# New places in the unit for the copy of the block ends and most other work of a Mamba scan stage

## The chip, the cores and the metric

The kernel runs on one core of a Trainium2 chip. The metric is the device time of one execution in microseconds. The core's engines each work through a queue of their own in order: PE (TensorE, matmuls), DVE (VectorE), ACT (ScalarE), POOL (GpSimd) and SP (SyncE, which issues DMAs here). They meet at semaphores.

## The reference

The input is (4, 2048, 256). A Mamba layer and a mixture of experts follow one another, each with a residual and a layer norm. The change is in the Mamba layer. Per batch, with 512 inner channels and 16 states:

```python
xz = x @ in_proj_w.T + in_proj_b;  x_in, z = split(xz)
x_conv = silu(causal_conv4(x_in) + conv_b)
dt_low, B, C = split(x_conv @ x_proj_w.T)          # 64, 16, 16
dt = softplus(dt_low @ dt_proj_w.T + dt_proj_b)
A_bar = exp(dt * A);  B_bar = (A_bar - 1) / A * B  # A = -exp(A_log)
h = A_bar * h + B_bar * x_conv                     # over 2048 positions
y = (sum_s h * C + D * x_conv) * silu(z)
x = layernorm(x + y @ out_proj_w.T + out_proj_b)
```

Then each token's router scores choose two of 16 experts.

## The kernel before, in words

The scan stage runs over 16 units. A unit is 512 positions of one batch; the state `h` is carried between units of the same batch. The 512 channels are 4 chunks of 128 partitions. A unit has 64 items, one for each chunk and state, in 32 pairs: pair `i`, half `e` is chunk `i // 16 * 2 + e`, and the state follows from `i % 16`. Item number `m = 2 i + e` is also the step of the unit. Each engine's program is a loop over `m` from 0 to 63; in each step it emits the item's fixed work and then whatever the tables put there. The tables are the whole schedule: no planner runs, and an instruction placed at a step waits by semaphore until its inputs are there, holding up all that is behind it on its engine.

There are two kinds of pairs (`KINDS`). For kind `d`, ACT makes `a_ps = exp(dt*A)` (`make_a`, L766), POOL makes `h = x_conv*b_rep` (`make_u`, L656), DVE multiplies the two (`make_b`, L1205) and scans (L1221). For kind `f`, PE makes the increments from turned rows and step matrices (`make_du`, L1050, four 128-column products a half) into the only `g_ps`, DVE corrects the starts of the four blocks of 128 (`join`, L1214) and scans (L1229). Then `hc = h*c_rep` is made on POOL (L673, one pair later) or, for three of 16 pairs, on DVE (L1239). PE adds it into `y_ps` two pairs later (`add_item`, L1028).

Beside its items a unit makes the next one's inputs, tile by tile, through the two PSUM banks `work`; the tiles take turns in the order of `PLACE`, and a tile waits until the one before it in its bank has been copied out. `x0` to `x3` and `z0` to `z3` are the input projection, `c0` to `c3` the convolution, `low` and `bc` are dt_low, B and C, `d0` to `d3` the dt projection, `T0` to `T3` turned `x_conv`, `r` the skip term, `o` the output projection of the unit before, `t`, `lg`, `pf` its transposition, logits and slot numbers. PE makes a tile at its step in `PLACE` (a part a step); ACT copies it one step after its last part (DVE for `r` and `o`). Softplus is Abs and Relu of a `d` tile, Sigmoid (`Z_AT`), Square and two polynomials in `g_ps` (`SQUARES_AT` on ACT, `LOGS_AT` on DVE), and an addition (`ADD_RELU_AT` on POOL), in two groups of two chunks; `PAUSE` is where the kinds leave `g_ps` free for it.

The block ends: B's rows leave `low` for DRAM (`store_rows` at SP step `BC_OUT_AT`), and come back spread over the partitions as `b_rep` and `c_rep`, as `b_part` and `c_part`, and as `b_end`, the ends of the four blocks (`load_parts` at `PARTS_AT`, L527 to L531). ACT copies `b_end` with its sign changed (`turn_ends`, L793, at `TURN_AT`), POOL multiplies it (`ENDS_AT`) for the joins of the next unit, and `both` (`BOTH_AT`) from the parts for the skip term. SP's program steps once a pair and issues the `c_rep` load of the pair after next when `hc` of two pairs ago is done. The load of the next unit's `x_t` waits for the gate (`GATE_AT`, Silu of all `z`).

Of the kernel before, what the change touches and what calls it, by code (L numbers as in the profile page):

```python
# [168 lines left out]
def mamba(nc, d):  # L169
# [5 lines left out]
    with ExitStack() as ctx:  # L175
        def sb(name, shape, dt=F32):
            return ctx.enter_context(nc.sbuf_tensor(name, shape, dt))
# [50 lines left out]
        low = sb("low", [RANK + 2 * NS, T])  # L228
# [108 lines left out]
        def pool_slot(s):  # L337
# [11 lines left out]
        NEXT = ["x0", "x1", "x2", "x3", "c0", "c1", "c2", "c3", "low", "bc", "d0", "d1", "T0", "T1", "z0", "z1"]  # L349
        OWN = ["d2", "d3", "T2", "T3", "r0", "r1", "r2", "r3", "z2", "z3"]  # L350
        ROUTING = ["o0", "o1", "t0", "t1", "lg", "pf"]
        PLACE = [("x0", 0), ("x1", 0), ("d2", 2), ("d3", 3), ("c0", 6), ("c1", 6), ("T2", 10), ("T3", 14), ("o0", 16), ("o1",
# [3 lines left out]
        U_AT = [-4, -1, None, 3, None, 6, 9, None, 10, None, 15, 17, 18, None, 24, None, 28, 32, None, 34, None, 38, 39, None,  # L356
                42, None, 47, 51, 53, None, 56, None]
        A_AT = [-2, 1, -1, 4, 6, 6, 9, 11, 11, 14, 16, 17, 19, 21, 27, 26, 29, 31, 31, 35, 37, 41, 42, 44, 44, 45, 51, 53, 55,
                56, 58, 57]
        DU_AT = [None, None, 2, None, 6, None, None, 10, None, 13, None, None, None, 24, None, 27, None, None, 34, None, 38,  # L360
                 None, None, 43, None, 48, None, None, None, 56, None, 58]
        SCATTER_AT = (1, 2, 4, 6, 9, 12, 13, 16)
        ADD_RELU_AT = (58, 63, 24, 26)
        Z_AT = (49, 5)
        STEPS_AT = (47, 48, 54, 57, 58, 61)
        SUMS_AT = (23, 24)
        SILU_AT = (12, 36)
        SQUARES_AT = ((51, 54, 55), (12, 18, 21))
        LOGS_AT = ((54, 55), (22, 24))
        TURN_AT, ENDS_AT, BOTH_AT = 45, 55, 49  # L370
        MAX_AT, INDEX_AT, IDS_AT, CHOOSE_AT, CANDIDATES_AT, REDUCE_AT, PLACES_AT, NOTED_AT = 45, 48, 50, 52, 55, 55, 59, 62
        ROOT_AT, INVERSE_AT, NORMALISE_AT = 24, 26, 28
        GATE_AT, HALO_IN_AT, HALO_OUT_AT = 59, 5, 61
        SKIP_AT = (25, 29, 35, 39)
        TOKENS_AT, ROWS_OUT_AT, BC_OUT_AT, PARTS_AT = 9, 23, 21, 23
        WHERE = dict(PLACE)
        ORDER = {t: n for n, (t, _) in enumerate(PLACE)}

# [3 lines left out]
        class Plan:  # L382
# [3 lines left out]
            def __init__(self, kinds, offset, per=0):  # L386
                self.tiles = [t for t, _ in PLACE if t in kinds]
                self.offset, self.per = offset, per
# [26 lines left out]
        last = Plan(OWN + ROUTING, AHEAD + INNER * (UNITS - 1))  # L415
        assert INNER % 2 == 0 and len(PLACE) == INNER
        assert min(WHERE["T0"], WHERE["T1"]) > WHERE["pf"]
# [154 lines left out]
        def _(pool):  # L572
# [85 lines left out]

            U_PLACE = sorted((U_AT[i] + e, i, e) for i in range(PAIRS) for e in range(2) if plain(i))

# [41 lines left out]
            def unit_program(u, plan):  # L702
                for m in range(ITEMS):
# [17 lines left out]
                    if m == ENDS_AT and plan is not last:  # L721
                        find_ends(u)
                    if m in ADD_RELU_AT:
                        c = ADD_RELU_AT.index(m)
                        if c >= 2:
                            add_relu(u, c)
                        elif plan is not last:
                            add_relu(later(u), c)
                    if plan is not second and m in SCATTER_AT:
                        scatter(u, SCATTER_AT.index(m))  # L730

# [13 lines left out]
        def _(act):  # L745
# [4 lines left out]

            A_PLACE = sorted((A_AT[i] + e, i, e) for i in range(PAIRS) for e in range(2))

# [173 lines left out]
            def weave(u, plan, m):  # L926
# [11 lines left out]
                for t in plan.whole_at(m - 1):  # L938
                    if t[0] != "o":
                        tile(u, plan, t)  # L940
                if plan.has("c0") and m in SILU_AT:
                    half = 2 * SILU_AT.index(m)
                    emptied_all(act, plan, u, [f"c{c}" for c in (half, half + 1)])
# [4 lines left out]
                if plan.has("d2"):  # L948
                    if m == Z_AT[1]:
                        find_z(u, 1)  # L950
                    if m in SQUARES_AT[1]:
                        squared(u, 1, SQUARES_AT[1].index(m))
                if plan.has("d0"):
                    if m == Z_AT[0]:
                        find_z(n, 0)
                    if m in SQUARES_AT[0]:
                        squared(n, 0, SQUARES_AT[0].index(m))
                    if m == TURN_AT:
                        turn_ends(u)
                    if m in STEPS_AT:  # L960
                        make_steps(u, plan, STEPS_AT.index(m))
                if m == GATE_AT:
# [41 lines left out]
        def _(pe):  # L1004
# [132 lines left out]

            DU_PLACE = [(DU_AT[i] + e, i, e) for i in range(PAIRS) for e in range(2) if not plain(i)]

# [28 lines left out]
        def _(dve):  # L1168
# [158 lines left out]
            def weave(u, plan, m):  # L1327
# [15 lines left out]
                if plan.has("o0"):  # L1343
                    if m in SUMS_AT:
                        norm_sums(u, plan, f"o{SUMS_AT.index(m)}")
                    if m == INVERSE_AT:
# [814 lines left out]
```

## Time and profile before

| what | us |
|---|---|
| median of 3 runs (2834.14 to 2836.39) | 2834.33 |
| the profiled execution | 2841.85 |
| its span, first to last instruction | 2840.0 |
| scan stage, up to about | 2425 |
| mean granted clock of TensorE, share of full | 0.956 |

The page gives the busy time of each engine; a timeline lists single instructions with the idle time of their engine before them and what ended it. The stage after 2425 us (the experts) is not touched.

### The profile page before, as it was taken

The numbers are of one execution on the slowest core, as the hardware profiler recorded it, in microseconds if no ns is written. First come the engines' busy times: TensorE is split into PE (matmuls) and PEld (weight loads), VectorE is DVE, ScalarE is ACT, GpSimd is POOL, SyncE is SP. The second block draws the span as 40 slices with busy tenths as digits, with TensorE's granted clock in tenths as the row PEclk, the third lists the DMA queues.
The fourth block names the chain that finished last, engine by engine and source line by source line (L and its number), as shares of the span: only waits on it lengthen the run. The fifth ranks groups of instructions, "written<-read, shape, count | busy, mean of one in ns | idle before, by whom it ended". The sixth has DMA issues, their size and how long they took to land. (4 is left out here: it accounts for less than half of the span.)

```text
span 2840.0 us, 37945 instructions
## 1 busy us (share of the span) xinstructions
PE 2558.9 (90%) x9658; PEld 1453.0 (51%) x9659; DVE 2363.1 (83%) x3895; ACT 1800.2 (63%) x3530; POOL 2284.4 (80%) x2094
## 2 busy tenths in 40 slices
PE   6889999999999999999898989898989988499997
PEld 2445554545454545455454545454545444377764
DVE  3889898989898989989897989898989889366668
ACT  5676766767676768585867676767676754133348
POOL 1889898979798989898998989898989898255553
PEclk8999999999999999999999999999999988699998
DMA  3333333433344333334333343434333332766557
GB/s 85 93 106 119 100 120 102 124 100 125 95 121 110 113 113 113 115 110 115 110 108 109 110 112 113 115 115 107 119 108 119 99 111 89 208 186 185 183 185 248
DMA packets 248306, 349.34 MB, mean 123 GB/s; under 512 B 75575, under 2 KB 123323, under 8 KB 247612
## 3 DMA queue, kind: packets, MB, share of 16 engines
q1 hardware_dynamic: 231372, 301.41, 36.4%
q0 software_dynamic: 15600, 44.79, 4.5%
q10 hardware_dynamic: 1152, 1.06, 0.2%
q8 instruction: 71, 1.16, 0.2%
q14 instruction: 111, 0.91, 0.1%
HBM read 288.72 MB, written 58.45 MB: 122 GB/s over the span
## 5 line engine op out<-in xcount | busy, mean ns | idle before, releaser
L673 POOL TENSOR_TENSOR hc<-h,c_rep 128x512 f32<-128x512 f32 x832 | 1053.1, 1271 | 165.9 <-PE y_ps L1028 87.7
L1028 PE MATMUL y_ps<-hc,dg_inv 128*128 128x512 f32 x1664 | 870.2, 616 | 25.2 <-POOL hc L673 22.3
L656 POOL TENSOR_TENSOR h<-x_conv,b_rep 128x512 f32<-128x512 f32 x640 | 807.6, 1271 | 86.5 <-DVE h L1221 60.1
L1221 DVE TENSOR_TENSOR_SCAN h<-a_ps,carry,h 128x512 f32<-128x512 f32 x640 | 807.0, 1272 | 12.6 <-ACT score L824 10.5
L766 ACT ACTIVATE a_ps<-dt,a_mat 128x512 f32<-128x512 f32 x640 | 436.5, 685 | 482.9 <-DVE h L1221 469.0
L1050 PEld LDWEIGHTS g_ps<-b_steps,x_conv_rows 128*128 128x128 f32 x3072 | 411.2, 199 | 278.3 <-issue 278.3
L1205 DVE SCALAR_TENSOR_TENSOR h<-a_ps,h 128x512 f32<-128x512 f32 x640 | 429.7, 672 | 72.2 <-ACT a_ps L766 65.8
L1050 PE MATMUL g_ps<-b_steps,x_conv_rows 128*128 128x128 f32 x3072 | 431.2, 285 | 45.6 <-DVE h L1229 17.8
L1028 PEld LDWEIGHTS y_ps<-hc,dg_inv 128*128 128x128 f32 x1664 | 291.2, 194 | 309.8 <-issue 203.8
L766 ACT ACTIVATE h<-dt,a_mat 128x512 f32<-128x512 f32 x384 | 269.9, 711 | 2.1 <-POOL hc L673 1.4
L1103 PE MATMUL work<-x_in,dg_tap 128*128 128x512 f32 x512 | 250.0, 593 | 1.9 <-ACT x_in L894 1.1
L1229 DVE TENSOR_TENSOR_SCAN g_ps<-g_ps,carry,h 128x512 f32<-128x512 f32 x192 | 246.8, 1286 | 5.4 <-ACT h L766 0.8
L1229 DVE TENSOR_TENSOR_SCAN h<-g_ps,carry,h 128x512 f32<-128x512 f32 x192 | 245.1, 1277 | 3.8 <-ACT h L766 0.3
L1720 POOL DMA_INDIRECT y_planes<-gathered,home x144 | 139.8, 971 | 132.0 <-DVE gathered L2051 120.4
L1028 PE MATMUL y_ps<-hc,ident 128*128 128x512 f32 x384 | 203.1, 619 | 8.0 <-DVE hc L1239 8.0
L1090 PE MATMUL work<-x_t,w_in 128*128 128x512 f32 x256 | 136.5, 641 | 44.1 <-DMA x_t<-in_x_t 30.8
L1214 DVE TENSOR_TENSOR g_ps<-g_ps,minus_u 128x6 f32<-128x6 f32 x192 | 31.4, 163 | 154.9 <-PE g_ps L1050 148.2
L1851 PE MATMUL banks<-w_up,gathered 128*128 x576 | 150.3, 384 | 0.0
L1239 DVE SCALAR_TENSOR_TENSOR hc<-g_ps,a_inv,c_rep 128x512 f32<-128x512 f32 x192 | 142.5, 742 | 0.0
L1114 PE MATMUL work<-low,dt_out 64*128 64x512 f32 x128 | 87.9, 772 | 60.4 <-ACT dt L866 58.9
L638 POOL DMA_INDIRECT slot_rows<-x_tok,place x120 | 121.5, 1013 | 25.0 <-issue 12.3
L1103 PEld LDWEIGHTS work<-x_in,dg_tap 128*128 128x128 f32 x512 | 91.0, 190 | 89.2 <-issue 87.5
(248 smaller groups left out, 3622.7 us busy)
## 6 DMA issues: line engine op xcount, KB each, us to landing
c_rep<-bc_rows SPq DMA_DIRECT2D x512, 256.0 KB, 3.4
b_rep<-bc_rows SPq DMA_DIRECT2D x320, 256.0 KB, 3.7
gathered<-slot_rows SPq DMA_DIRECT2D x144, 129.5 KB, 2.2
gathered<-y_planes SPq DMA_DIRECT2D x32, 512.0 KB, 5.6
x_t<-in_x_t SPq DMA_DIRECT2D x16, 512.0 KB, 5.0
x_tok<-in_x_tok SPq DMA_DIRECT2D x16, 512.0 KB, 4.9
out<-mixed_rows SPq DMA_DIRECT2D x16, 512.0 KB, 3.1
x_t_rows<-y_gated SPq DMA_DIRECT2D x15, 512.0 KB, 5.7
```

What stands on the lines that cost most here:

```text
L656: nc.gpsimd.tensor_tensor(h[:, i % SLOTS, e], x_conv[:, u[1] % 2, chunk(i, e)], b_rep[:, n % BS], ALU.mult).then_inc(u_ready, 1)
L673: nc.gpsimd.tensor_tensor(hc[:, i % HCS, e], h[:, i % SLOTS, e], c_rep[:, i % CS], ALU.mult).then_inc(hc_pool, 1)
L766: nc.scalar.activation(out, dt[:, c], ACT.Exp, scale=a_mat[:, c, s:s + 1]).then_inc(made, 1)
L1028: nc.tensor.matmul(y_ps[:, e], by, hc[:, i % HCS, e], start=first_one, stop=(i % HALF == HALF - 1)).then_inc(summed, 1)
L1050: one = nc.tensor.matmul(g_ps[:, e, k * P:(k + 1) * P], x_rows[:, c, k], b_steps[:, f, k], start=True, stop=True)
L1103: mm = nc.tensor.matmul(out, dg_tap[:, c, k], x_in[:, c, k:k + T], start=(k == 0), stop=(k == TAPS - 1))
L1205: nc.vector.scalar_tensor_tensor(out=slot, in0=a_ps[:, e], scalar=1.0, in1=slot, op0=ALU.subtract, op1=ALU.mult).then_inc(b_ready, 1)
L1221: nc.vector.tensor_tensor_scan(slot, a_ps[:, e], slot, before_it, ALU.mult, ALU.add).then_inc(scanned, 1)
L1229: nc.vector.tensor_tensor_scan(out, g_ps[:, e], slot, before_it, ALU.add, ALU.mult).then_inc(scanned, 1)
L1239: nc.vector.scalar_tensor_tensor(out=hc[:, i % HCS, e], in0=g_ps[:, e], scalar=a_inv[:, c, s:s + 1], in1=c_rep[:, i % CS], op0=ALU.mult, o ...
L1720: nc.gpsimd.indirect_dma_start(d["y_planes"], bass.IndirectOffsetOnAxis(home[:, c:c + 1], 0), y_slots[:, c], None).then_inc(y_stored[c // ...
L1851: one = nc.tensor.matmul(gu_ps[:, c % 2, 0:2 * IF], xt[:, c % 4, h * P:(h + 1) * P], w_up[:, e, h], start=(h == 0), stop=(h == KT - 1))
```

## The change

No work is added or removed. The tables that say at which step of the unit an operation is emitted get other numbers: `PLACE` for PE's tiles and so their order in the two banks, `U_AT`, `A_AT`, `DU_AT` for the operands of the pairs, and nearly every single step. With them go the waits.

```diff
-        PLACE = [("x0", 0), ("x1", 0), ("d2", 2), ("d3", 3), ("c0", 6), ("c1", 6), ("T2", 10), ("T3", 14), ("o0", 16), ("o1",
-                 17), ("x2", 22), ("r0", 24), ("x3", 25), ("r1", 26), ("c3", 27), ("c2", 31), ("r2", 34), ("t0", 36), ("t1", 36),
-                 ("r3", 39), ("low", 39), ("lg", 40), ("d1", 46), ("bc", 46), ("d0", 47), ("z2", 50), ("pf", 52), ("z1", 52),
-                 ("z3", 54), ("z0", 54), ("T0", 61), ("T1", 61)]
-        U_AT = [-4, -1, None, 3, None, 6, 9, None, 10, None, 15, 17, 18, None, 24, None, 28, 32, None, 34, None, 38, 39, None,
-                42, None, 47, 51, 53, None, 56, None]
-        A_AT = [-2, 1, -1, 4, 6, 6, 9, 11, 11, 14, 16, 17, 19, 21, 27, 26, 29, 31, 31, 35, 37, 41, 42, 44, 44, 45, 51, 53, 55,
-                56, 58, 57]
-        DU_AT = [None, None, 2, None, 6, None, None, 10, None, 13, None, None, None, 24, None, 27, None, None, 34, None, 38,
-                 None, None, 43, None, 48, None, None, None, 56, None, 58]
-        SCATTER_AT = (1, 2, 4, 6, 9, 12, 13, 16)
-        ADD_RELU_AT = (58, 63, 24, 26)
-        Z_AT = (49, 5)
-        STEPS_AT = (47, 48, 54, 57, 58, 61)
-        SUMS_AT = (23, 24)
-        SILU_AT = (12, 36)
-        SQUARES_AT = ((51, 54, 55), (12, 18, 21))
-        LOGS_AT = ((54, 55), (22, 24))
-        TURN_AT, ENDS_AT, BOTH_AT = 45, 55, 49
-        MAX_AT, INDEX_AT, IDS_AT, CHOOSE_AT, CANDIDATES_AT, REDUCE_AT, PLACES_AT, NOTED_AT = 45, 48, 50, 52, 55, 55, 59, 62
-        ROOT_AT, INVERSE_AT, NORMALISE_AT = 24, 26, 28
-        GATE_AT, HALO_IN_AT, HALO_OUT_AT = 59, 5, 61
-        SKIP_AT = (25, 29, 35, 39)
-        TOKENS_AT, ROWS_OUT_AT, BC_OUT_AT, PARTS_AT = 9, 23, 21, 23
+        PLACE = [("x0", 1), ("x1", 1), ("c0", 4), ("c1", 4), ("T3", 7), ("d3", 9), ("T2", 11), ("d2", 11), ("o0", 14), ("o1",
+                 18), ("x2", 22), ("r0", 25), ("x3", 25), ("r1", 27), ("c3", 29), ("c2", 30), ("t1", 35), ("t0", 36), ("r2", 37),
+                 ("low", 39), ("r3", 43), ("bc", 44), ("lg", 44), ("d0", 47), ("d1", 48), ("z1", 50), ("pf", 51), ("z0", 52),
+                 ("z3", 54), ("T0", 56), ("z2", 58), ("T1", 62)]
+        U_AT = [-3, -1, None, 0, None, 6, 9, None, 10, None, 15, 20, 22, None, 24, None, 27, 31, None, 33, None, 36, 38, None,
+                42, None, 47, 50, 51, None, 56, None]
+        A_AT = [-3, 1, 1, 3, 4, 7, 10, 13, 12, 15, 17, 18, 22, 24, 26, 25, 29, 33, 33, 36, 39, 40, 42, 43, 46, 47, 50, 53, 55,
+                55, 57, 58]
+        DU_AT = [None, None, 2, None, 5, None, None, 11, None, 14, None, None, None, 24, None, 29, None, None, 34, None, 38,
+                 None, None, 44, None, 48, None, None, None, 57, None, 59]
+        SCATTER_AT = (1, 2, 5, 6, 8, 9, 14, 15)
+        ADD_RELU_AT = (57, 58, 26, 29)
+        Z_AT = (50, 14)
+        STEPS_AT = (47, 48, 55, 57, 62, 63)
+        SUMS_AT = (22, 24)
+        SILU_AT = (17, 34)
+        SQUARES_AT = ((51, 54, 55), (16, 19, 20))
+        LOGS_AT = ((54, 55), (22, 23))
+        TURN_AT, ENDS_AT, BOTH_AT = 52, 55, 48
+        MAX_AT, INDEX_AT, IDS_AT, CHOOSE_AT, CANDIDATES_AT, REDUCE_AT, PLACES_AT, NOTED_AT = 48, 49, 50, 51, 54, 56, 59, 62
+        ROOT_AT, INVERSE_AT, NORMALISE_AT = 29, 29, 30
+        GATE_AT, HALO_IN_AT, HALO_OUT_AT = 60, 1, 60
+        SKIP_AT = (25, 26, 39, 43)
+        TOKENS_AT, ROWS_OUT_AT, BC_OUT_AT, PARTS_AT = 8, 23, 23, 24
```

## Rows read from the trace of the kernel before

**Rows 1.** The page: busy us (share of the span) and instructions of each engine.

```profile
PE 2558.9 (90%) x9658; PEld 1453.0 (51%) x9659; DVE 2363.1 (83%) x3895; ACT 1800.2 (63%) x3530; POOL 2284.4 (80%) x2094
```

**Rows 2.** Windows of a unit: length, busy PE, PEld, DVE, ACT, POOL, clock, DMA.

```profile
212.30:359.80 147.50, 138.47 (x507) 74.32 (x506) 130.59 (x185) 103.19 (x197) 131.09 (x118) 0.97 0.38 112
...
950.10:1097.60 147.50, 137.80 (x509) 74.31 (x508) 130.80 (x184) 103.15 (x197) 130.87 (x118) 0.98 0.38 112
```

**Rows 3.** The line of the root: durations in ns, first and last start.

```profile
L891 ACT ACTIVATE spread<-spread x15: 205/205/208, 267.6 to 2333.4; 128x4 f32<-128x4 f32 x15
```

**Rows 4.** Table of waits, whole span: us in total, times, longest.

```profile
DVE g_ps L1214 <- PE g_ps L1050: 148.2, 51, 9.7
...
PE work L1090 <- DMA x_t<-in_x_t: 30.8, 14, 2.3
```

**Rows 5.** Timeline of DVE, one unit: start, us, instruction, idle before.

```profile
1015.45 0.17 DVE L1214 TENSOR_TENSOR g_ps<-g_ps,minus_u 128x6 f32<-128x6 f32 x1 [0.74 <-PE g_ps L1050]
...
1049.32 1.28 DVE L1221 TENSOR_TENSOR_SCAN h<-a_ps,carry,h 128x512 f32<-128x512 f32 x1 [0.70 <-ACT score L824]
...
1056.32 1.26 DVE L1221 TENSOR_TENSOR_SCAN h<-a_ps,carry,h 128x512 f32<-128x512 f32 x1
1065.58 0.17 DVE L1214 TENSOR_TENSOR g_ps<-g_ps,minus_u 128x6 f32<-128x6 f32 x1 [8.00 <-PE g_ps L1050]
...
1093.47 0.69 DVE L1205 SCALAR_TENSOR_TENSOR h<-a_ps,h 128x512 f32<-128x512 f32 x1 [2.42 <-ACT a_ps L766]
...
1095.92 0.69 DVE L1205 SCALAR_TENSOR_TENSOR h<-a_ps,h 128x512 f32<-128x512 f32 x1 [0.55 <-ACT a_ps L766]
```

**Rows 6.** Timeline of PE in the same unit.

```profile
1051.32 1.12 PE L1114 MATMUL work<-low,dt_out 64*128 64x512 f32 x2
...
1057.84 2.07 PE L1114 MATMUL work<-low,dt_out 64*128 64x512 f32 x2 [3.35 <-ACT dt L866]
...
1090.12 2.74 PE L1028 MATMUL y_ps<-hc,dg_inv 128*128 128x512 f32 x6
1095.18 1.96 PE L1090 MATMUL work<-x_t,w_in 128*128 128x512 f32 x4 [2.32 <-DMA x_t<-in_x_t]
```

**Rows 7.** Timeline of ACT in the same unit.

```profile
1051.27 0.70 ACT L766 ACTIVATE h<-dt,a_mat 128x512 f32<-128x512 f32 x1
1055.71 0.22 ACT L793 ACTIVATE b_minus<-b_end 128x24 f32<-128x24 f32 x1 [3.74 <-DMA b_end<-bc_rows]
...
1062.40 1.28 ACT L872 ACT_TABLE_LOAD   x1
1063.69 1.15 ACT L872 ACTIVATE x_arg<-x_arg,shifts 128x1024 f32<-128x1024 f32 x1
...
1087.88 1.91 ACT L966 ACTIVATE gate<-gate 128x2048 f32<-128x2048 f32 x1
...
1095.19 0.69 ACT L766 ACTIVATE a_ps<-dt,a_mat 128x512 f32<-128x512 f32 x1 [0.66 <-POOL dt L700]
```

**Rows 8.** Timeline of SP's DMA issues in the same unit.

```profile
1049.82 0.67 SPq L531 DMA_DIRECT2D b_end<-bc_rows  x1
...
1089.89 0.43 SPq L540 DMA_DIRECT2D x_t<-in_x_t  x1
```

**Rows 9.** Of the tile `b_end`: from issue to landing.

```profile
DMA to landing us min/median/max: 4.1/5.8/7.1
```

**Rows 10.** Window of the slow stretch, columns as in rows 2.

```profile
1057.80:1063.40 5.60, 5.56 (x12) 3.02 (x13) 0.00 (x0) 5.24 (x14) 5.60 (x6) 0.50 0.08 28
```

**Rows 11.** Timeline of POOL in the same unit.

```profile
1050.68 1.27 POOL L673 TENSOR_TENSOR hc<-h,c_rep 128x512 f32<-128x512 f32 x1 [0.46 <-DVE h L1221]
...
1093.90 1.26 POOL L700 TENSOR_TENSOR dt<-dt,poly 128x512 f32<-128x512 f32 x1
```

**Rows 12.** Groups of instructions in the window of rows 2: count, busy us, mean ns.

```profile
L673 POOL TENSOR_TENSOR hc<-h,c_rep 128x512 f32<-128x512 f32 x52 | 65.8, 1272 | 9.7 <-PE y_ps L1028 5.2 <-DVE h L1221 2.2 <-DVE h L1229 2.0
...
L1205 DVE SCALAR_TENSOR_TENSOR h<-a_ps,h 128x512 f32<-128x512 f32 x40 | 26.9, 671 | 4.1 <-ACT a_ps L766 3.8 <-POOL h L656 0.4
```

## The prediction

> **What bounds the kernel now.** I read the page's busy shares first [rows 1]: no engine is full, but three stand close together. The reader sees that more sharply in the windows of one unit [rows 2]: of 147.5 us, PE is busy 137.8, POOL 130.9, DVE 130.8 and ACT 103.2, and the other full units are within 3 us of that. A unit takes (2333.4 - 267.6) / 14 = 147.56 us, by the one square root in each [rows 3]; 64 steps, so 2.3 us a step. The scans sit on DVE and need all that the others make, so what a unit could lose is DVE's idle time, some 17 us of it.
>
> Then the table of waits [rows 4], to see who DVE waits for. One wait stands out: the join of the block starts (L1214) on PE, 148 us in total. The unit's timeline of DVE [rows 5] shows that it is one hole: after a scan at 1056.32 nothing until the join of pair 25 at 1065.58, 8.00 us idle. A second hole is at the unit's end, 2.42 and 0.55 us for `a_ps` (steps 62, 63). The rest are waits below 0.8 us.
>
> Back from the first hole: PE's timeline [rows 6] has `d0` at 1057.84, 3.35 us idle before it, waiting for ACT's copy of `d1` (same bank). ACT [rows 7] ends an exponential at 1051.97 and then sits 3.74 us until `b_end` has landed, because its copy, `TURN_AT` 45, is ahead of the copy of `d1` in its queue. SP [rows 8] could issue that load only at 1049.82, behind the store of `low`, and it takes 5.8 us to land (median, [rows 9]). Then comes a second price: the granted clock is 0.50, so 1.2 of 2.4 GHz [rows 10], and a product takes 2.07 us instead of 1.12; so PE's pairs of records in 1057.8 to 1063.4 give back 2.8 us late. Idle and slow clock together are 6.2 of the 8.0 us.
>
> **What the change takes away.** (a) `TURN_AT` 52. Its load moves too: the store goes from SP step 21 to 23, the parts from 23 to 24. SP gets to 24 when POOL has made `hc` of pair 22, which was 1050.68 + 1.27 = 1051.95; with two issues ahead `b_end` goes out near 1053.6 and lands near 1059.5. DVE's step 50 would without the hole begin at 1057.6, so the copy at step 52 comes 2 us or more after the landing. `low` is copied in step 43 as before, and `d0`, now ahead of `d1`, waits only for `bc`, copied at 45. POOL's `both` (now 48) needs the parts landed: POOL has three 1.27 us operations between, so 0 to 1.3 us of wait, in POOL's own idle time; I take 0. Removed: 8.00 us a unit. (b) `add_relu` of chunk 1 moves from POOL step 63, which ended at 1095.16 [rows 11] just ahead of ACT's exponential for pair 0 [rows 7], to 58, and `softplus` stays at 55: the 2.97 us at the unit's end go. (c) In steps 24 to 44 PE had no idle time and was late: DVE has six small waits there, 0.18 to 0.74 us, the largest for `du` of pair 15, 2.13 us in all (that one in [rows 5]). Now `softplus` ends one DVE step earlier (23 instead of 24), ahead of the sums of `o1`, so PE starts `du` of pair 13 some 5 us earlier against DVE. I take all 2.13. Together 13.1 us.
>
> **What it adds.** PE's steps are priced by its rows: an item or one 128x512 product 0.86 us (six records in 2.74, less 0.16 of overlap), a `du` 0.9, four transposes 0.45, `d` 1.05; DVE's by a scan 1.2 and a `make_b` 0.6 (mean duration less overlap) [rows 6, 12].
> 1. The gate goes to step 60, behind `z2` made at 58. SP loads `x_t` only after it (0.1 us after the Silu in the old order, [rows 7, 8]), 5.0 us to landing. From the scan of pair 29: 4.4 us of ACT, then 5.4, makes 9.8; DVE reaches step 0 after 7. `x0`, `x1` now stand at step 1, ahead of `du` of pair 2, and delay PE so that join 4 is late by 1.35 us. It was 2.3 us of harmless PE idle time [rows 4]. Bounds 0 and 2.8 (no step of lead).
> 2. `c0`, `c1` at 4, `T3` 7, `d3` 9, `T2`, `d2` 11. After `du` 4 PE has 13.4 us of work up to the end of `du` 7 (steps 11, 12 instead of 10, 11), DVE 11.3 us from join 4 to join 7; in the old order PE had 10.9. So 2.1 us. `T3` also waits for the copy of `c0`, which ACT makes in step 8; PE comes there as late as that. Bounds 0 (if PE keeps a lead) and 4.
> 3. ACT in steps 14 to 18: Sigmoid, Square, Silu and four table loads, 12 us against DVE's 9.6; join 7's wait gives ACT most of that. 0.3, bounds 0 and 2.4.
> 4. Root at ACT 29, inverse at DVE 29 (24 and 26 before). The root stands behind an exponential that waits for the scan of pair 14: 0.7 + 1.28 + 0.2 us after it, where DVE has one scan of 1.2 to do. 1.15 us; bounds 0 and 2.3.
> 5. At steps 48 to 50 PE has `d1` (1.05) between the halves of `du` 25, and it comes late: steps 24 to 47 hold 24 items, 10 halves of `du`, 14 products of `x`, `c` and `low`, `r0` to `r3`, `d0`, transposes, `bc` and `lg`, so PE is at step 48 about 51.7 us after the `softplus` of step 23, while DVE ends the scan of pair 23 after 50.0 (24 scans, 15 `make_b`, 4 `hc`, 5 joins, the sums of `o1`, four skips, two gated chunks, term 4). Join 25: 1.5 us, bounds 0 and 3. `MAX_AT` 48 waits for `lg`'s scores, made in ACT step 48, as before at 45 [rows 5]: 0.75 for 0.70.
> 6. Index 49, ids 50, choose 51, `pf` 51 stand back to back (before 48, 50, 52, 52): POOL waits about 2 us for the index, ACT's choose ends 4.8 us after it, PE waits 0.5 to 2.2 us at `pf`. Behind it are only items and `z` tiles; PE is then some 1 us ahead at join 29. 0 at full clock; upper bound in rival A.
> `SCATTER_AT` spreads over 1 to 15 instead of 1 to 16, POOL's 1.27 us operations [rows 12] are less crowded at 15 to 19: I take nothing.
> Sum: 1.35 + 2.1 + 0.3 + 1.15 + 1.5 + 0.05 = 6.45; with 13.1 removed, -6.65 a unit. Fifteen units have it (the last makes nothing for a next one), so -100; the prologue's copy no longer stands ahead of `d0`: -3. The profiled execution took 2841.85 us (1.85 beside its span of 2840.0), so it would take 2739. It is 7.5 over the median of the runs; from the median, 2834.3 - 103 = 2731.
>
> The trace bears on term 4: a table load starts at 1062.40 and its activation at 1063.69, 1.29 us for a switch [rows 7]. The Trainium skill ("ScalarE: Activation LUTs", *What ACT_TABLE_LOAD costs*) gives a switch 1283 ns for the load and another 1380 ns of drain. The load agrees, the drain isn't seen; by the page term 4 would be 2.5 us and the time some 20 us longer (an estimate from that page), 2752.
>
> **Rivals.**
> A. PE's new pause at `pf` or at `T3` makes the clock fall as after `d0`. For: that pause was 3.35 us, the new ones together reach 2 to 3. Against: after the 2.32 us before `x0` PE ran at full speed, four records in 1.96 us [rows 6]. Price 2.8 us for a slow stretch like [rows 10] and 1 for what it holds: -2.85 a unit, 2788.
> B. Slower. `x0` and `x1` stand ahead of `du` 2 and 4, and SP's `x_t` behind a gate one step later. If ACT comes to the gate 4.5 us or more later than I take, PE idles 6 us at `x0` and comes out at half clock: 4.5 + 2.8 = 7.3 us eats the gain. At three steps (6.9 us) of lateness it is 9.7 - 6.65 = +3.05 a unit, 2877. For: ACT's queue has carry, `z2`, load and Silu in one step. Against: ACT has the least work of the four.
> C. The copy still waits, since its load was moved too. It then holds ACT 3.7 us again, now ahead of pair 27's exponential: -2.95 a unit, 2787.
> D. The new waits overlap or vanish: -10.5 a unit, 2673. POOL's 130.9 us a unit would allow it.
> E. The idle time only moves: 2834.
>
> **Chances.** Forecast 0.54, A 0.17, B 0.12, C 0.06, D 0.08, E 0.03. A measurement of this kernel tells 0.2% (6 us) from no change. Faster 0.85, same 0.03, slower 0.12. The forecast's own range is 2700 to 2765; with A and C it is 2680 to 2800, which leaves out B, E and most of D.
>
> **What would show it.** A unit of 141 us by the roots; no idle time before the copy of the block ends; no half-clock stretch once a unit; DVE's wait before join 25 under 3 us; no `a_ps` wait over 1 us in steps 62 and 63. New: waits before joins 4 and 7, and before the inverse (L1288). I am wrong if the copy waits for its load, if the clock is low once a unit at another place, or if `x_t` holds PE by more than 4 us.

## The result, and the profile after

The changed kernel takes 2873.63 us (median of 4 runs, 2869.80 to 2874.85) beside 2835.36 for the kernel before on the same chip: ratio 1.0132, 95% interval 1.0114 to 1.0149. It is slower by 38 us; the prediction was 2731, with a range of 2680 to 2800. The profiled execution took 2873.16 us, its span 2871.3.

"Join 25" is the join of pair 25, "the softplus" DVE's first operation on the polynomials in `g_ps` (L1323, step 54), and PE's "pause" is idle time of PE in front of an instruction.

The page's busy line of after, which answers to [rows 1]: the number of instructions is the same on each of these engines, and PE's busy time is 24 us longer.

```profile
PE 2583.0 (90%) x9658; PEld 1464.8 (51%) x9659; DVE 2359.6 (82%) x3895; ACT 1808.6 (63%) x3530; POOL 2285.2 (80%) x2094
```

The line of the root (durations in ns, first and last start), for [rows 3]:

```profile
L891 ACT ACTIVATE spread<-spread x15: 205/207/208, 274.6 to 2377.3; 128x4 f32<-128x4 f32 x15
```

A unit is (2377.3 - 274.6) / 14 = 150.19 us, 2.63 longer than before where 6.65 less was forecast. Before the first root 7.0 us were added and after the last 12.6 taken away; five steps of that are the root's own new place. 7.0 + 14 x 2.63 - 12.6 = 31.3 is the difference of the spans. The prologue did gain: DVE's first scan starts at 62.5 in place of 69.5, so 7 us where 3 were forecast.

The timeline of DVE over one unit, those lines that have idle time before them (start, us, instruction, idle before and what ended it), for [rows 5]:

```profile
976.33 0.22 DVE L1237 TENSOR_SCALAR carry<-g_ps,minus_u 128x1 f32<-128x1 f32 x1 [0.72 <-PE y_ps L1028]
984.45 0.17 DVE L1214 TENSOR_TENSOR g_ps<-g_ps,minus_u 128x6 f32<-128x6 f32 x1 [1.59 <-PE g_ps L1050]
992.66 0.69 DVE L1205 SCALAR_TENSOR_TENSOR h<-a_ps,h 128x512 f32<-128x512 f32 x1 [0.61 <-ACT a_ps L766]
997.04 0.69 DVE L1205 SCALAR_TENSOR_TENSOR h<-a_ps,h 128x512 f32<-128x512 f32 x1 [2.48 <-ACT a_ps L766]
...
1019.61 0.69 DVE L1257 TENSOR_TENSOR skip<-work,x_conv 128x512 f32<-128x512 f32 x1 [1.65 <-PE work L1119]
1025.83 0.18 DVE L1288 RECIPROCAL spread<-spread 128x4 f32<-128x4 f32 x1 [1.16 <-ACT spread L891]
...
1059.74 0.17 DVE L1214 TENSOR_TENSOR g_ps<-g_ps,minus_u 128x6 f32<-128x6 f32 x1 [0.49 <-PE g_ps L1050]
1063.95 1.28 DVE L1221 TENSOR_TENSOR_SCAN h<-a_ps,carry,h 128x512 f32<-128x512 f32 x1 [0.36 <-ACT score L824]
1068.71 0.17 DVE L1214 TENSOR_TENSOR g_ps<-g_ps,minus_u 128x6 f32<-128x6 f32 x1 [1.29 <-PE g_ps L1050]
1073.16 0.69 DVE L1205 SCALAR_TENSOR_TENSOR h<-a_ps,h 128x512 f32<-128x512 f32 x1 [1.17 <-ACT a_ps L766]
1077.46 0.69 DVE L1205 SCALAR_TENSOR_TENSOR h<-a_ps,h 128x512 f32<-128x512 f32 x1 [0.46 <-ACT a_ps L766]
1084.58 1.22 DVE L1323 SCALAR_TENSOR_TENSOR poly<-g_ps,x_arg 128x1024 f32<-128x1024 f32 x1 [3.88 <-ACT g_ps L887]
1101.74 0.69 DVE L1205 SCALAR_TENSOR_TENSOR h<-a_ps,h 128x512 f32<-128x512 f32 x1 [2.33 <-ACT a_ps L766]
```

The hole of 8.00 us before join 25 is gone, 1.29 is left. In its place stand many smaller waits, above all 3.88 us before the softplus (step 54), 2.33 at the unit's end and 2.48 at step 19. With two of 0.21 us they are 18.6 us, against 15.2 counted in the same way before. Of these 3.4 us the unit shows 2.63, since DVE was also busy for 0.8 us less ([rows 2] and the windows below).

Back from the 3.88 us. The timeline of ACT:

```profile
1068.68 1.28 ACT L872 ACT_TABLE_LOAD   x1
1069.97 1.15 ACT L872 ACTIVATE x_arg<-x_arg,shifts 128x1024 f32<-128x1024 f32 x1
1071.14 1.28 ACT L766 ACT_TABLE_LOAD   x1
...
1074.78 0.31 ACT L923 ACTIVATE chosen<-y_gated 128x128 bf16<-128x128 f32 x1
...
1082.86 0.69 ACT L853 ACTIVATE gate<-work,b_in 128x512 f32<-128x512 f32 x1 [4.69 <-PE work L1094]
1083.44 1.11 ACT L887 ACTIVATE g_ps<-square,shifts 128x1024 f32<-128x1024 f32 x1
```

and the timeline of PE in the same stretch:

```profile
1075.23 0.68 PE L1010 MATMUL work<-ahead,dt_out 1*128 1x80 f32 x2 [3.20 <-ACT chosen L923]
...
1076.29 2.06 PE L1028 MATMUL y_ps<-hc,dg_inv 128*128 128x512 f32 x2
1078.14 1.91 PE L1094 MATMUL work<-x_t,w_in 128*128 128x512 f32 x2
```

The Sigmoid with its two table loads stands on ACT ahead of the chosen tokens, PE waits 3.20 us for these at `pf`, and comes out of the pause at the lower of its two clocks, 1.2 of 2.4 GHz: an item takes 2.06 us in place of 1.02. ACT waits 4.69 us for `z0`, and the squared term in `g_ps` (L887) that the softplus needs is queued behind that copy. In the kernel before, the pause at `pf` was 0.3 to 1.6 us (14.4 us over 15 times). A second pause sits before `x2`, which waits for DVE's norm sum:

```profile
1005.80 1.13 PE L1090 MATMUL work<-x_t,w_in 128*128 128x512 f32 x2 [3.46 <-DVE x_tok L1272]
1006.76 1.73 PE L1028 MATMUL y_ps<-hc,ident 128*128 128x512 f32 x2
```

The windows of the unit and of both stretches (busy PE, PEld, DVE, ACT, POOL; then the granted clock), for [rows 2, 10]:

```profile
953.94:1104.13 150.19, 139.14 (x507) 74.90 (x508) 129.96 (x184) 103.42 (x197) 130.41 (x118) 0.97 0.37 110
1075.20:1083.40 8.20, 8.17 (x22) 4.02 (x23) 5.05 (x7) 3.51 (x8) 3.15 (x5) 0.58 0.23 78
1005.80:1010.20 4.40, 4.40 (x7) 1.90 (x8) 4.36 (x9) 2.67 (x6) 2.83 (x3) 0.63 0.10 34
```

The table of waits over the span (us in total, times, longest) shows that both are in every unit:

```profile
ACT gate L853 <- PE work L1094: 63.7, 14, 4.7
...
PE work L1090 <- DVE x_tok L1272: 48.2, 14, 3.5
```

### The profile page after: what moved, and what is told of

Read it like the earlier page. It is cut to its first block and busy times, and to the rows that moved or that the text cites. A ratio compares the mean times of both kernels' runs of the same rounds, so it can differ in the third digit from the quotient of the medians.

```text
span 2871.3 us, 37946 instructions
## 1 busy us (share of the span) xinstructions
PE 2583.0 (90%) x9658; PEld 1464.8 (51%) x9659; DVE 2359.6 (82%) x3895; ACT 1808.6 (63%) x3530; POOL 2285.2 (80%) x2094
## 3 DMA queue, kind: packets, MB, share of 16 engines
q8 instruction: 71, 1.16, 0.2%
## 5 line engine op out<-in xcount | busy, mean ns | idle before, releaser
L1028 PE MATMUL y_ps<-hc,dg_inv 128*128 128x512 f32 x1664 | 884.5, 623 | 40.2 <-POOL hc L673 24.1
L1050 PEld LDWEIGHTS g_ps<-b_steps,x_conv_rows 128*128 128x128 f32 x3072 | 403.1, 195 | 240.7 <-issue 236.9
L1028 PEld LDWEIGHTS y_ps<-hc,dg_inv 128*128 128x128 f32 x1664 | 299.7, 197 | 343.6 <-issue 210.0
L1050 PE MATMUL g_ps<-b_steps,x_conv_rows 128*128 128x128 f32 x3072 | 418.4, 280 | 26.3 <-DVE carry L1237 13.6
L1103 PE MATMUL work<-x_in,dg_tap 128*128 128x512 f32 x512 | 244.2, 596 | 2.9 <-ACT x_in L837 2.9
L1028 PE MATMUL y_ps<-hc,ident 128*128 128x512 f32 x384 | 221.0, 661 | 16.9 <-DVE hc L1239 16.5
L1090 PE MATMUL work<-x_t,w_in 128*128 128x512 f32 x256 | 147.7, 685 | 74.2 <-DVE x_tok L1272 48.2
L1094 PE MATMUL work<-x_t,w_in 128*128 128x512 f32 x256 | 147.8, 664 | 0.9 <-ACT dt L866 0.9
L784 ACT ACTIVATE carry<-h,minus_u 128x1 f32<-128x1 f32 x192 | 45.9, 286 | 157.5 <-DVE h L1229 157.5
```

Source lines behind the costliest of these rows:

```text
L1028: nc.tensor.matmul(y_ps[:, e], by, hc[:, i % HCS, e], start=first_one, stop=(i % HALF == HALF - 1)).then_inc(summed, 1)
L1050: one = nc.tensor.matmul(g_ps[:, e, k * P:(k + 1) * P], x_rows[:, c, k], b_steps[:, f, k], start=True, stop=True)
L1090: mm = nc.tensor.matmul(out, w_in[:, k, m * P:(m + 1) * P], x_t[:, nq, k], start=(k == 0), stop=(k == KT - 1))
L1094: mm = nc.tensor.matmul(out, w_in[:, k, m * P:(m + 1) * P], x_t[:, src, k], start=(k == 0), stop=(k == KT - 1))
L1103: mm = nc.tensor.matmul(out, dg_tap[:, c, k], x_in[:, c, k:k + T], start=(k == 0), stop=(k == TAPS - 1))
```

## The experiments

Medians are of 4 to 10 runs; ratios are to the kernel before, measured beside each (2834.0 to 2834.9), with their 95% interval. B is the kernel before, A the kernel after. Some edits are shown shortened to the numbers that change. Waits of DVE are those of one middle unit, where nothing else is said; the units of one execution are not all alike.

**The copy of the block ends alone (B).**

```diff
-        TURN_AT, ENDS_AT, BOTH_AT = 45, 55, 49
+        TURN_AT, ENDS_AT, BOTH_AT = 52, 55, 49
```

> The kernel before with one number changed: TURN_AT 45 becomes 52. If the 8.0 us hole before join 25 is the price of the copy that waits for its load (theory of the prediction, step a), some 7 to 8 us of each of 15 units go: 2720 us, no half-clock stretch once a unit. Rival: other waits stand right behind the hole (PE, POOL and ACT are each within 12% of the unit) and refill it: less than 3 us a unit, 2790 us or more.

2786.55 us, 0.9835 (0.9819 to 0.9852). The timeline of DVE where the hole was:

```profile
1031.80 0.17 DVE L1214 TENSOR_TENSOR g_ps<-g_ps,minus_u 128x6 f32<-128x6 f32 x1 [1.77 <-PE g_ps L1050]
1035.06 0.69 DVE L1205 SCALAR_TENSOR_TENSOR h<-a_ps,h 128x512 f32<-128x512 f32 x1 [1.75 <-ACT a_ps L766]
1046.94 1.23 DVE L1323 SCALAR_TENSOR_TENSOR poly<-g_ps,x_arg 128x1024 f32<-128x1024 f32 x1 [3.12 <-ACT g_ps L887]
```

The run gains 47 us, 7 of them in the prologue, and a unit is 144.58 us by the roots, 2.98 shorter. The unit shown is one of the long ones (145.4 us). The waits of 1.77 us (join 25) and 1.75 us (the exponential of pair 26) stand in all 14 units, but the one before the softplus is 3.1 to 3.2 us in three, 1.6 to 1.8 in ten and absent in one: 1.9 on average. So of a hole of 8.1 us on average (7.5 to 9.8) some 5.4 come back. PE now pauses 2.70 us at `pf`, where in the kernel before it paused 0.8 in the same unit: the pause at `pf` grows when the hole in front of it goes, with the table's numbers for `pf`, the Sigmoid and choose as they were. Its length is the same in every unit; what follows is not. In a unit with the long wait, then in the one without any:

```profile
1038.69 0.68 PE L1010 MATMUL work<-ahead,dt_out 1*128 1x80 f32 x2 [2.70 <-ACT chosen L923]
...
1039.75 2.05 PE L1094 MATMUL work<-x_t,w_in 128*128 128x512 f32 x2
...
896.27 0.41 PE L1010 MATMUL work<-ahead,dt_out 1*128 1x80 f32 x2 [2.69 <-ACT chosen L923]
...
896.91 1.10 PE L1094 MATMUL work<-x_t,w_in 128*128 128x512 f32 x2
```

The unit in which PE stayed at full clock has no wait before the softplus and took 142.4 us. As far as this one unit shows, what costs here is the slow clock behind the pause, and not the pause.

**`add_relu` alone (B).**

```diff
-        ADD_RELU_AT = (58, 63, 24, 26)
+        ADD_RELU_AT = (58, 59, 24, 26)
```

> The kernel before with one number changed: the addition of chunk 1 at POOL step 59 instead of 63. Step b of the prediction gave it the whole 2.97 us at the unit's end: 2790 us. Rival, from the trace read again: the first 2.42 us wait for ACT, which comes from the gate's Silu (1.91) and a table load (1.28) and not from POOL; only the 0.66 us before the second exponential are POOL's: 2826 us, and the 2.4 us wait in step 62 or 63 stays.

2860.04 us, 1.0097 (1.0080 to 1.0114): slower. The 0.55 us of step 63 went, the 2.42 of step 62 stayed at 2.41. The timeline of PE at the unit's end shows the cost:

```profile
1093.19 1.12 PE L1028 MATMUL y_ps<-hc,dg_inv 128*128 128x512 f32 x2 [0.77 <-POOL hc L673]
1096.75 3.75 PE L1090 MATMUL work<-x_t,w_in 128*128 128x512 f32 x4 [2.43 <-DMA x_t<-in_x_t]
```

POOL's extra 1.27 us at step 59 makes `hc` late, PE pauses for it, then 2.43 us for `x_t`, and the products of `x0` take 3.75 us; in the same unit before, after the pause for `x_t` alone, 1.96 [rows 6]. DVE then waits 2.68 us for PE's sum in `y_ps` (step 3) and 1.53 before join 4 (0.39 before). Both pauses are in all 14 units, but the slow clock is not: in six the four records of `x0` take 1.96 us. Between two roots there are 147.0 to 147.9 us where `x0` ran at full clock, 148.8 to 150.3 where it did not. In the kernel before, two of 14 units had a slow `x0` (3.65 us), with no pause for `hc` ahead.

**`pf` behind `z0` (A).**

```diff
-  ("z1", 50), ("pf", 51), ("z0", 52), ...   CANDIDATES_AT 54
+  ("z1", 50), ("z0", 51), ("pf", 53), ...   CANDIDATES_AT 55
```

> The changed kernel with pf at 53 behind z0 (at 51), and the candidates at 55. Theory: PE's 3.2 us pause at pf, for ACT's choose that stands behind Sigmoid and two table loads, drops the clock, z0 is late, ACT waits 4.7 us for it ahead of the Square, and softplus makes DVE wait 3.9 us. With two products in front of pf the pause is under 1 us, the clock stays up there, and 4 us a unit go: 2813 us. Rival: the Square is late through ACT's own queue, so DVE's wait before softplus stays over 3 us and the time within 10 us of 2873.

2814.95 us, 0.9936 (0.9917 to 0.9956), 58.7 below A, or 3.9 a unit. The pause at `pf` is 1.19 us and the item behind it takes 1.10; the wait of 3.88 is gone (those for pairs 26 and 27, 1.18 and 0.33, are not):

```profile
1056.91 0.44 PE L1010 MATMUL work<-ahead,dt_out 1*128 1x80 f32 x2 [1.19 <-ACT gate L853]
...
1057.58 1.10 PE L1028 MATMUL y_ps<-hc,ident 128*128 128x512 f32 x2
```

**The first Silu at 9 (A), alone and with `pf` at 53.**

```diff
-        SILU_AT = (17, 34)
+        SILU_AT = (9, 34)
```

> The changed kernel with the first Silu of x_conv at step 9 instead of 17. Theory: between steps 14 and 18 ACT has Sigmoid, Square, Silu and four table loads and is late for the exponentials of pair 10, DVE waits 0.6 and 2.5 us; with Silu and its two loads at a step where ACT is free these 3.1 us go: 2827 us. Rival: PE (join 7, x2) or POOL sets the pace in steps 14 to 24 and takes the time back: 2865 us or more.

2833.32 us, 0.9994 (0.9980 to 1.0007), 40.3 below A. Waits of 0.61 and 2.48 became 0.85, a new one of 1.97 stands at step 11, and PE's pause before `x2` fell to 1.1 us. Units took from 146.8 to 149.9 us. PE's timeline at `pf`, first in a unit of 149.8 us, then in one of 146.8:

```profile
1064.87 0.67 PE L1010 MATMUL work<-ahead,dt_out 1*128 1x80 f32 x2 [3.19 <-ACT chosen L923]
...
1065.92 2.05 PE L1028 MATMUL y_ps<-hc,dg_inv 128*128 128x512 f32 x2
...
1213.27 0.41 PE L1010 MATMUL work<-ahead,dt_out 1*128 1x80 f32 x2 [3.19 <-ACT chosen L923]
...
1213.91 1.10 PE L1028 MATMUL y_ps<-hc,dg_inv 128*128 128x512 f32 x2
1214.85 1.68 PE L1094 MATMUL work<-x_t,w_in 128*128 128x512 f32 x2
```

The pause is 3.19 us in both. In the first PE starts at half clock, in the second it falls back one item later (granted clock in the windows of the two stretches: 0.58 and 0.78), and the softplus waits 3.88 and 2.31 us. So of this wait some 1.6 us are the clock's and 2.3 are left without it, in A's order. The other difference between the two units is of the same kind, at step 35. Both have the pause of 1.01 us before the item there, and only the first a slow stretch behind it:

```profile
1028.23 1.13 PE L1028 MATMUL y_ps<-hc,dg_inv 128*128 128x512 f32 x2 [1.01 <-DVE y_gated L1251]
...
1031.83 1.91 PE L1050 MATMUL g_ps<-b_steps,x_conv_rows 128*128 128x128 f32 x8
...
1178.13 1.13 PE L1028 MATMUL y_ps<-hc,dg_inv 128*128 128x512 f32 x2 [1.01 <-DVE y_gated L1251]
...
1181.20 1.05 PE L1050 MATMUL g_ps<-b_steps,x_conv_rows 128*128 128x128 f32 x8
```

Joins 20 and 23 wait 1.00 and 1.21 us in the first unit, and only 0.50 (join 23) in the second: with the softplus 3.3 us of waits for the 3.0 of the units.

> The kernel after with both single edits together: pf at 53 behind z0 (alone 2815.0 us, 58.7 less than after) and the first Silu at 9 in place of 17 (alone 2833.3 us, 40.3 less). Theory (the two crowdings sit at different places of the unit and don't cover each other): they add, 2873.6 - 58.7 - 40.3 = 2775 us. Rival (one slack feeds both, PE's lead): 2805 to 2815 us. The unit with the Silu alone took 146.8 us in some units and 149.8 in others; if the clock after pf was what made the difference, the units here are all alike, near 143.3 us.

2797.91 us, 0.9868 (0.9851 to 0.9884): the Silu adds 17.0 us to `pf`'s gain, not 40.3. Between theory and rival. Alone the Silu's move had also brought the wait before the softplus from 3.7 to 2.8 us on average, for the clock fell later in many units, and the other edit removes that wait by itself; and the waits of 1.00 and 1.21 us at joins 20 and 23 are here too in some units (145.8 us, the others 144.3).

**The copy put back, with `pf` at 53 (A).**

```diff
-        TURN_AT 52, BC_OUT_AT 23, PARTS_AT 24
+        TURN_AT 45, BC_OUT_AT 21, PARTS_AT 23
```

> The kernel after with pf at 53, and the copy of the block ends put back: the copy at 45, SP's store of low at 21 and the load of the parts at 23. It tells what the copy is worth once nothing behind it waits. Theory (in the kernel before it was worth 3 us a unit of its 8.00, because the pause at pf took the rest): here the hole of 8 us comes back in full, less the waits that it covers (1.29 before join 25, 1.18 and 0.33 for exponentials behind it): 5.2 us a unit and the prologue's 7 us, so 2815 + 15 x 5.2 + 7 = 2900 us. Rival (the copy is worth 3 us a unit wherever it stands): 2815 + 48 = 2863 us.

2899.34 us, 1.0227 (1.0210 to 1.0244): 84.4 above the run without it. The theory had 85, but not by what happened: no hole of 8 us comes back before join 25. The copy now waits 7.28 us for its load, where it was 3.74 in B, and DVE pays 4.19 us of that at step 46, with 1.43 us for the scores (0.36 without the edit). The timeline of ACT:

```profile
1081.42 0.22 ACT L793 ACTIVATE b_minus<-b_end 128x24 f32<-128x24 f32 x1 [7.28 <-DMA b_end<-bc_rows]
```

In B the copy was worth 47 us. The two numbers don't measure one thing with and without the pause at `pf`: the edits differ (the store and the load go with the copy here) and so does the copy's own wait.

**Root, inverse and second skip put back (A).**

```diff
-        ROOT_AT, INVERSE_AT, NORMALISE_AT = 29, 29, 30    SKIP_AT[1] 26
+        ROOT_AT, INVERSE_AT, NORMALISE_AT = 24, 26, 28    SKIP_AT[1] 29
```

> The kernel after with pf at 53, and root, inverse and normalise put back to 24, 26 and 28 (after: 29, 29, 30), the second skip to 29 (after: 26). DVE's waits of 1.50 us for r1 (step 26) and of 1.16 us before the inverse (step 29) in a unit should go. Theory (each of these waits is paid in full): 2815 - 15 x 2.66 = 2775 us. Rival (PE is behind DVE in these steps, so that DVE, coming earlier, waits at the joins behind, pair 15 above all, for PE's du): 2800 to 2815 us, with a wait of 1 to 2.6 us before a join of steps 30 to 50.

With `pf` at 53: 2810.07 us, 0.9920 (0.9903 to 0.9936), 4.9 less. Waits of 1.50 and 1.16 us went, and 1.08 before the first skip and 2.40 before join 15 came. The rival's range.

> The kernel after with pf at 53, the first Silu at 9 (together 2797.9 us), and root, inverse, normalise at 24, 26, 28 and the second skip at 29. With the Silu at 17 that last step gave only 5 us (2815.0 to 2810.1) of the 40 that its waits held: DVE then waited 2.40 us before join 15, PE being late from a pause of 3.46 us before x2 and the half clock behind it. With the Silu at 9 that pause is 1.1 us and there is no half clock. Theory (PE's pause at x2 was what made it worthless): here the waits of 0.82 and 1.16 us are paid in full, 2797.9 - 15 x 1.9 = 2769 us. Rival (PE is late in steps 24 to 30 whatever the clock): 2790 to 2798 us, with 1.5 us or more before join 15.

With the Silu too: 2777.50 us, 0.9802 (0.9785 to 0.9819), 20.4 less. Without the Silu's move the table of waits has the line of A for the pause before `x2` (48.2 us, 14 times, longest 3.5); with it:

```profile
PE work L1090 <- DVE x_tok L1272: 15.3, 14, 1.1
```

Join 15 still waits 1.42 us, so 20 and not 28. The same edit was worth 0.3 us a unit while PE came late out of the pause at `x2`, and 1.4 once it did not.

**Copy at 52 and `pf` at 53 (B).**

```diff
-  ("z2", 50), ("pf", 52), ("z1", 52), ...   TURN_AT 45
+  ("z2", 50), ("z1", 52), ("pf", 53), ...   TURN_AT 52
```

> The kernel before with the copy of the block ends at 52 and pf moved from 52 (ahead of z1) to 53 (behind it). The run with the copy alone took 2786.6 us and had a new DVE wait of 3.12 us for ACT's Square (step 54) in each unit; behind it stood PE's pause of 2.70 us at pf for ACT's chosen tokens, and the half clock after it. Theory (the pause at pf is what ate the copy's 8.00 us): z1 covers 1.7 us of the pause, the clock stays up, the wait of 3.12 us goes: 2786.6 - 15 x 3.0 = 2741 us, and a unit of 141.0 us. Rival (the time only moves to the next late wait, of ACT's exponentials for pair 26, 1.75 us and growing): 2775 to 2790.

2763.31 us, 0.9748 (0.9731 to 0.9764), 23 below the copy alone. The wait before the softplus went in every unit, and 0.8 came back before join 4 in most. The waits of 1.77 and 1.75 us (join 25, pair 26) are unchanged: they have nothing to do with `pf`.

**Three more edits on top of that (B, copy 52, `pf` 53).**

The gate alone, the first two `b_steps` alone, and both.

```diff
-        GATE_AT, HALO_IN_AT, HALO_OUT_AT = 59, 5, 61
+        GATE_AT, HALO_IN_AT, HALO_OUT_AT = 57, 5, 61
```

```diff
-        STEPS_AT = (47, 48, 54, 57, 58, 61)
+        STEPS_AT = (52, 53, 54, 57, 58, 61)
```

> The kernel before with the copy at 52, pf at 53 (together 2763.3 us) and the gate's Silu at 57 in place of 59, so that SP's load of x_t goes out two steps earlier. In that run PE idled 2.40 us at x0 for the transfer of x_t, the eight products of x0 and x1 then took 4.7 us in place of 3.8, and DVE waited 1.19 us before join 4. Theory (x_t is late because the Silu is): PE's idle time at x0 goes, the clock stays up, join 4 waits under 0.4 us: 2763.3 - 15 x 0.8 = 2751 us, or 2739 if the a_ps waits of 2.42 and 0.81 us at the unit's end shrink too, being at other steps. Rival (ACT has no room at 57: the exponentials of pairs 29 to 31 wait for the Silu there, by as much as those of pair 0 did at 59): 2760 to 2770 us.

2828.49 us, 0.9967 (0.9953 to 0.9981), 65 slower than without it. `x_t` is in time, but the Silu with its loads now stands ahead of the exponential of pair 30. DVE waits 3.88 us for that and 3.33 at step 63 (2.42 and 0.81 before). The scan before the next `du` is late with it, and PE pauses 3.77 us and comes out at half clock:

```profile
1076.97 2.05 PE L1050 MATMUL g_ps<-b_steps,x_conv_rows 128*128 128x128 f32 x8 [3.77 <-DVE h L1229]
1078.81 3.55 PE L1028 MATMUL y_ps<-hc,dg_inv 128*128 128x512 f32 x4
```

> The kernel before with the copy at 52, pf at 53 (together 2763.3 us) and ACT's first two b_steps (1.28 us each) at 52 and 53 in place of 47 and 48. They stand ahead of the Sigmoid whose two table loads delay the exponential of pair 26, for which DVE waits 1.75 us in step 50. Theory (ACT's crowd of steps 47 to 51 sets that wait): the Sigmoid starts 1.3 to 2.5 us earlier, the wait of 1.75 goes or falls below 0.5: 2763.3 - 15 x 1.3 = 2744 us. Rival (ACT is as crowded at 52 to 54, with choose, the Square and the z copies): the wait reappears before the softplus or the exponential of pair 27, 2755 to 2770 us.

2762.22 us, 0.9751 (0.9732 to 0.9770): no change. The wait of 1.75 us fell to 0.59, but ACT's copy of a `z` tile is later, and PE's pause for it is now 2.08 us (1.2 before), followed by four products in 3.60 us:

```profile
1178.59 3.60 PE L1094 MATMUL work<-x_t,w_in 128*128 128x512 f32 x4 [2.08 <-ACT gate L853]
```

Join 29 then waits 1.27 us, where there was no wait. So 1.2 of the 1.75 us before pair 26 were those of two `b_steps` ahead of its exponential in ACT's queue.

> The two edits of the runs beside it together. Theory (they sit at different places of the unit): the gains add, 2763.3 - 12 - 19 = 2732 us, or 2720 if the gate's own waits shrink. Rival (PE, busy 137 of 143 us of a unit, is the bound once the waits are down to this): no unit under 142 us, 2750 us.

2825.52 us, 0.9974 (0.9963 to 0.9984): as with the gate alone.

**Who makes the 2.42 us at the unit's end.** The last `b_steps` from 61 to 63, in B alone, then on top of the copy, `pf` and the first two `b_steps`, and then with `ADD_RELU_AT[1]` 62 in place of 63.

```diff
-        STEPS_AT = (47, 48, 54, 57, 58, 61)
+        STEPS_AT = (47, 48, 54, 57, 58, 63)
```

> The kernel before with one edit: ACT's b_steps of step 61 (1.26 us, between the gate's Silu and the table load for the exponential of pair 0) at 63. The prediction put DVE's 2.42 us at the unit's end down to POOL's add_relu; moving that alone took away only the 0.55 us of step 63. Theory (the wait is ACT's chain of load, Silu, carries, b_steps, load): it falls by 1.27 to 1.15 us, 2834.3 - 15 x 1.27 = 2815 us if DVE is given it. Rival (x_t and PE set the start of the unit, DVE only waits elsewhere): 2828 to 2834 us, with the 1.27 us before join 4 or step 63.

2835.89 us, 1.0003 (0.9994 to 1.0013): no change. The wait at step 62 is 1.25 in place of 2.42, the one at 63 1.73 in place of 0.55.

> The kernel before with the copy at 52, pf at 53, the first two b_steps at 52 and 53 (together 2762.2 us) and the last b_steps at 63 in place of 61. Theory: the wait at step 62 falls by 1.27 us, 2762.2 - 19 = 2743 us. Rival (PE, coming from its wait for x_t, is late for join 4 by the same time): 2755 to 2762 us.

2760.86 us, 0.9732 (0.9716 to 0.9748): the same shift, 0.69 and 2.06 us.

> The same with POOL's add_relu of chunk 1 at 62 in place of 63: half 1 of pair 0's exponential waits 1.0 us for it. Theory (that wait is paid once the 2.42 us are shorter): 6 to 12 us below the run beside it, so 2734 us. Rival (an earlier add_relu delays hc on POOL and PE pauses for it just ahead of x_t, comes out at half clock, as with add_relu at 59 in the kernel before, which then took 2860.0 us): 2765 to 2785 us.

2750.99 us, 0.9706 (0.9690 to 0.9722), the best version found, 83 us below B and 123 below A. The timeline of DVE at the unit's end:

```profile
1052.98 0.69 DVE L1205 SCALAR_TENSOR_TENSOR h<-a_ps,h 128x512 f32<-128x512 f32 x1 [1.25 <-ACT a_ps L766]
```

The wait has two makers in a row: ACT's chain of Silu, `b_steps` and table load, and POOL's `add_relu` 1.2 us behind it. With ACT's part alone moved, the wait passed to POOL's and the time stayed; with POOL's moved as well 10 us went. POOL's at 62 without ACT's wasn't run. Join 4 is at 1.54 us now, so PE is next.

## Why the prediction was wrong

The ledger of a unit, from the two timelines of DVE. Forecast: 15.2 - 13.1 + 6.45 = 8.6 us of waits; measured 18.6.

| step of the prediction | forecast | measured |
|---|---|---|
| (a) copy | -8.00 | the wait gone, and the three below marked * in its place |
| (b) `add_relu` | -2.97 | -0.64 (2.33 is left) |
| (c) small waits, 24 to 44 | -2.13 | -1.71, and 1.65 for `r1` |
| 1. join 4 | +1.35 | none (0.39 before); 0.72 at step 10 |
| 2. join 7 | +2.1 | 1.59 |
| 3. ACT, steps 14 to 18 | +0.3 | 3.09, where 0.78 was |
| 4. root and inverse | +1.15 | 1.16, paid only if PE keeps up |
| 5. joins 23, 25*, score | +1.55 | 0.49, 1.29, and -0.34 for the score |
| 6. choose and `pf`* | 0 | 3.88 |
| no term: pairs 26, 27* | 0 | 1.63 |

The waits are 10 us a unit above the forecast. Of 12 us too much, 3.88 stand at the softplus and 1.63 at pairs 26 and 27, which the prediction had at nothing; 2.33 are left of step (b), 2.0 of step 3 and 2.1 of step (c). The other steps took 1.8 us less than forecast, join 4 above all.

The largest is step 6. The prediction saw PE's pause at `pf`, put it at 0.5 to 2.2 us, and said that only items and `z` tiles were behind it. It was 3.20, since ACT's choose stood behind a switch to Sigmoid and back (1.28 us for a load, 1.15 for the Sigmoid, 1.28 for a load), and ACT's copy of `z0` carries the term for the softplus behind it in the queue. Shown by `pf` at 53: -58.7 us, 3.9 a unit, where 2813 was expected and 2815 came; with it the changed kernel is faster than the one before. That the switch makes the pause is read from ACT's rows; no run moved the Sigmoid or choose alone. This is rival A's mechanism. Its price was right for this one pause, 2.8 us for a slow stretch and 1 for what it holds, 3.8 together, and its 2788 missed because the other steps failed too. The prediction's argument against it was a single unit, in which PE ran at full clock after 2.32 us before `x0`. The same trace has two units of 14 in which it did not, after 2.19 us at 357.10 and after 2.30 here:

```profile
800.85 3.65 PE L1090 MATMUL work<-x_t,w_in 128*128 128x512 f32 x4 [2.30 <-DMA x_t<-in_x_t]
```

And most of that pause doesn't come from the new places of index, ids and choose, as step 6 has it: with `TURN_AT` alone changed it is already 2.70.

Step (a) had the cause of the hole right (in the changed kernel ACT doesn't wait before the copy of the block ends, so rival C is out too) and its worth wrong. I read the hole as idle time that goes when its cause goes. In B 5.4 of 8.1 us came back in three waits: 1.77 at join 25, 1.75 for ACT's exponential of pair 26, and 1.9 on average before the softplus. Only the last is the pause at `pf`: with `pf` at 53 it goes and the others stay as they are. Of these three the prediction had booked join 25 alone (term 5).

Step (b) took the releaser of the wrong wait. In B the exponential of half 0, for which DVE waits 2.42 us, started right behind ACT's own work, with no idle time:

```profile
1091.46 1.28 ACT L766 ACT_TABLE_LOAD   x1
1092.75 0.69 ACT L766 ACTIVATE a_ps<-dt,a_mat 128x512 f32<-128x512 f32 x1
```

Only half 1 shows POOL [rows 7]. I put the 2.42 and the 0.55 together and gave both to POOL.

Step 3 was mis-sized: 12 us of ACT against 9.6 of DVE, of which I let join 7 take most. From 985.6 to 996.3 ACT had no idle time, with four table loads, Sigmoid, Square and Silu, and DVE waited 3.09 us, 2.3 more than before: the upper bound of 2.4 was nearly reached and 0.3 taken. DVE late by this was also late with the norm sum, hence the pause of 3.46 us before `x2`, which no step of the prediction had. Putting the Silu at 9 gave 40 us, 17 with `pf` at 53.

In step (c) four of the six small waits went (two of 0.21 us are still there), and DVE waited 1.65 us for `r1`, which stands behind the slow stretch after `x2`. With the Silu at 9, where that stretch is gone, it waits 0.83.

Steps 2, 4 and 5 came out within 0.6 us; of their mechanisms only that of step 4 was tried. Rival B named 2877, and 2874 came, but that is luck: `x_t` held PE 0.8 us a unit (11.1 us over 14), less than the 2.2 of before [rows 4]. Of the signs of being wrong that the prediction gave, the one that came true is the low clock once a unit at another place, and it did so at two, `pf` and `x2`.

Of what A loses, three edits give back 58.7 + 17.0 + 20.4 = 96.1 us (2873.6 to 2777.5). The 14 us from there to B with copy and `pf` (2763.3) weren't taken apart; A has waits of 1.97 us at step 11 and 1.07 before join 7 that B hasn't.

The switch itself was as forecast, 1.29 us from load to Sigmoid (1068.68 to 1069.97), and none of the drain that the Trainium skill ("ScalarE: Activation LUTs", *What ACT_TABLE_LOAD costs*) adds to it is seen: the load starts as the `carry` before it ends (1068.68). By an estimate from that page `chosen` would come 2.8 us later, for two switches; the rows decide.

## What to carry to other kernels

Before a long wait is booked as gain, list what comes next in the same stretch without it, on each engine: behind the hole of 8 us stood three waits, of PE, of ACT, and for a pause of PE that only grew once the hole was gone, and they took 5.4 back. Look at every unit before one of them stands for all; units of one execution differed by 3 us here. In a schedule where PE has under 10 us of slack a unit [rows 2], a pause of PE can cost the half clock behind it as well as itself, so an edit elsewhere (a POOL addition, a set of ACT scalings) is first priced by what it does to PE's pauses. And take the releaser from the instruction that ends the wait, not from its neighbour.

## What the hardware showed

The clock after a pause of PE was not the same function of the pause each time. What ran at 1.2 GHz behind it, by the lengths of the records:

| pause of PE | run | slow behind it |
|---|---|---|
| 3.20 us at `pf` | after | from the first item on in 13 of 14 units |
| 3.19 us at `pf` | `a_silu9` | from the first item on in 7 of 14, from a later one in the others |
| 2.70 us at `pf` | copy alone | in 13 of 14 units |
| 2.08 to 2.51 us before `x0`, 0.5 to 0.8 shortly ahead | `b_relu59` | in 8 of 14, three of them in full (3.75 us for 1.96) |
| 2.04 to 2.32 us before `x0` | before | in 2 of 14 (after 2.19 and 2.30) |
| 0.3 to 1.6 us at `pf` | before | in 1 of 14 (after 1.58) |
| 1.19 to 1.36 us at `pf` | `a_pf53` | in none of 14 |

Two pauses of 3.19 us, and two of 1.01, at the same places of one execution, came out differently, which made units of 149.8 and 146.8 us of the same instructions. So a pause tells how likely the fall is, and not whether it comes. What else decides is not settled here.

One more: two makers of one wait. The two halves of DVE's wait at the unit's end passed 1.2 us from one to the other, with no change in time, until ACT's 1.26 us and POOL's addition were both moved.
